# Combining two expert outputs per token: rows ordered by partition, second choice scaled on ScalarE

## The chip, the cores and the metric

The kernel is one program on one core of a Trainium2 chip. The metric is the device time of one execution in microseconds (us). A core has TensorE (PE in the profile), VectorE (DVE), ScalarE (ACT), GpSimd (POOL) and SyncE (SP), which run in parallel and meet at semaphores, and 16 DMA engines that move data between the chip's memory and the on-chip buffer of 128 partitions. SP, ScalarE and GpSimd issue the transfers.

## What is computed

The input `x` holds 128 sequences of 64 tokens with 128 channels, 8192 tokens in all, in float32. Two layers run over it, each an attention block and a feed-forward block with residuals. The change touches the end of the last block only, a mixture of 8 experts of which each token takes 2:

```python
gate_scores = jax.nn.softmax(x @ Wg + bg, axis=-1)
topk_scores, topk_idx = jax.lax.top_k(gate_scores, TOP_K)          # TOP_K = 2
topk_scores = topk_scores / (jnp.sum(topk_scores, axis=-1, keepdims=True) + 1e-08)
combine_w = jnp.einsum('bsk,bske->bse', topk_scores, onehot)
for e in range(NUM_EXPERTS):
    h = jax.nn.gelu(x @ W1[e] + b1[e])
    y = h @ W2[e] + b2[e]
    output = output + y * combine_w[..., e:e + 1]
...
x = x + output
```

Since only two of the eight weights of a token differ from zero, the kernel computes two rows of 128 outputs per token and adds them, each times its gate, to the token.

## The kernel before

Tokens live in 64 tiles of 128 (one token per partition), in 16 groups of `GT` = 4 tiles. `s.xg(g)` is the resident copy of group g, 128 partitions by 4 tiles by 128 channels in float32 (256 KB). Four stages follow each other, each closed by a barrier of all engines:

- `load_weights` and `first_layer`, to about 400 us.
- `cross_attention`, the longest stage. Beside the attention, it routes: for each group it finds the two best experts of each token and writes the normalised token twice (choice 0 and choice 1) into `moe_slots`, by indirect DMAs on GpSimd, sorted by expert. Each slot row also carries `dest`, an integer that says which row of the later output buffer belongs to this token and choice. VectorE steps `dest` once per group (line 1083), starting from a table of constants, `C_DST` (line 66, used in line 1093).
- `apply_experts`: 71 tiles of 256 slots go through the two products of their expert. SP loads a tile of slots (up to 12 ahead; before it reuses a buffer, it waits until the old tile's outputs have landed, line 1325), TensorE, ScalarE and VectorE compute, and GpSimd writes the 256 output rows of 512 bytes to `s.z` (`moe_outputs`, 16384 rows by 128 float32, 8.39 MB) with two indirect DMAs (line 1334), at the row that `dest` gives. Slots without a token carry a number beyond the buffer and are not written.
- `combine`, the last stage: for each of the 16 groups SP loads the rows of both choices from `s.z` into one of four buffers `f_z` (two DMAs of 256 KB, line 1467). VectorE does eight `scalar_tensor_tensor` (x = z * gate + x, 128 by 128 each, line 1483): four for choice 0, a `drain` (line 1485), because the next four read what these wrote, and four for choice 1. The last one counts `combined` up. ScalarE computes nothing in this stage; it waits for `combined` and issues the store of the group (256 KB, line 1473). SP waits for `combined` of group g-4 before it refills that group's buffer.

In memory the row of choice k, tile t, partition p is row (64k + t) * 128 + p. So a partition's load for one choice of a group is four pieces of 512 bytes, each 64 KB from the next, and neighbouring partitions lie side by side. The order of the work in `combine` is written out by hand: each engine runs its loop over the groups in sequence.

Of the kernel before, what the change touches and what calls it, by code (L numbers as in the profile page):

```python
# [10 lines left out]
ALU = mybir.AluOpType  # L11
ACT = mybir.ActivationFunctionType
AX = mybir.AxisListType

P = 128
BATCH, SEQ, D = 128, 64, 128
TILES = BATCH * SEQ // P
GT = 4
GROUPS = TILES // GT
# [11 lines left out]
C_TRI, C_ONE, C_DST, C_IT, C_R0, C_N0 = 1001, 1129, 1257, 1385, 1457, 1465  # L31
# [3 lines left out]
def constants():  # L35

    t, s = np.arange(SEQ), np.arange(SEQ // 2)
    w = 2 * np.pi / SEQ
    re = np.cos(w * np.outer(t, s))
    im = -np.sin(w * np.outer(t, s))  # L40
    im[:, 0] = (-1.0) ** t
    straight, turned = np.concatenate([re, im], 1), np.concatenate([im, re], 1)
    c, n = 2 * np.cos(w * np.outer(s, t)), 2 * np.sin(w * np.outer(s, t))
    a, b = c.copy(), c.copy()
    a[0], b[0] = 1.0, (-1.0) ** t
    inv, inv_turned = np.concatenate([a, b], 0) / SEQ, np.concatenate([n, -n], 0) / SEQ
    out = np.zeros((P, C_ALL))
    for u in range(2):
        here, other = slice(64 * u, 64 * u + 64), slice(64 * (1 - u), 64 * (1 - u) + 64)
        out[here, C_DQ + 64 * u:C_DQ + 64 * u + 64] = straight  # L50
        out[other, C_DK + 64 * u:C_DK + 64 * u + 64] = straight
        out[other, C_DK + P + 64 * u:C_DK + P + 64 * u + 64] = turned
        out[here, C_INV + 64 * u:C_INV + 64 * u + 64] = inv
        out[here, C_INV + P + 64 * u:C_INV + P + 64 * u + 64] = inv_turned
    out[:, C_ID:C_ID + P] = np.eye(P)
    ch = np.arange(P)
    by_parity = np.argsort(ch // 8 % 2, kind="stable")
    out[:, C_HM:C_HM + P] = ch[:, None] // 8 == by_parity[None, :] // 8

    out[ch, C_ROW + ch % 8 * 8 + ch // 16] = 1  # L60
    out[:, C_IE:C_IE + 32] = np.repeat(np.arange(8), TOP)[None]
    out[:, C_I8:C_I8 + 8] = np.arange(8)[None]
    out[:, C_DC] = ch % 8 + 64
    out[:, C_TRI:C_TRI + P] = ch[:, None] < ch[None, :]
    out[:, C_ONE:C_ONE + P] = 1
    out[:, C_DST:C_DST + 2 * TILES] = np.arange(2 * TILES)[None] * P + ch[:, None]
    out[:, C_IT:C_IT + 72] = np.arange(72)[None]
    out[:, C_R0:C_R0 + 8] = np.arange(8)[None] * BATCH * SEQ
    out[0, C_N0:C_N0 + 8] = np.arange(8) * BATCH * SEQ
    return out.astype(np.float32)  # L70
# [778 lines left out]
def cross_attention(nc, s, ctx_in, picks, tab):  # L849
# [4 lines left out]
    m = {n: sem("c_" + n) for n in names.split()}  # L854
# [4 lines left out]
    with ExitStack() as ctx:  # L859
# [144 lines left out]
        def _(dve):  # L1004
            def step(i, k):
# [74 lines left out]
                    dve.tensor_tensor(mask[:], eq[:, 0, :, :], eq[:, 1, :, :], ALU.add).then_inc(mr["mask"], 1)  # L1080
                if (g := group(i, k, ROUTE_STEP)) is not None:
                    wait(dve, scattered, 128 * g)
                    dve.tensor_scalar(dest, dest, GT * P, None, ALU.add)
                if (g := group(i, k, ROUTE_TOP)) is not None:
                    dve.drain()
                    for j in range(GT):
# [1 line left out]
                if (g := group(i, k, ROUTE_POS)) is not None:  # L1088
# [1 line left out]
                    dve.drain()  # L1090
                    dve.tensor_reduce(pf[:], pk[:], AX.X, ALU.add).then_inc(mr["pos"], 1)
                    dve.tensor_tensor(crun[:], crun[:], picked[:], ALU.add)
            dve.tensor_scalar(dest, s.dst_rows.rearrange("p (k t) -> p k t", k=2)[:, :, 0:GT], float(-GT * P), None, ALU.add)
            dve.tensor_copy(crun[:], s.count0)
            dve.memset(one8[:], 1.0)
            dve.memset(zero[:], 0.0)
# [187 lines left out]
def attend_and_route(nc, s, ctx_in, out):  # L1284

    sem = s.sem
    names = "x_t xt2 h gelu h_high h_split y y_done exp combined stored"
    m = {n: sem("d_" + n) for n in names.split()}
    x_in = [sem(f"d_x_in{n}") for n in range(XBUF)]
    y_out = [sem(f"d_y_out{n}") for n in range(YBUF)]  # L1290
# [161 lines left out]

def combine(nc, s, m, z_in, sb, gate, out):

    zt = [sb(f"f_z{n}", [P, 2, GT, D]) for n in range(4)]
    ov = out.rearrange("(t two) s d -> (two s) t d", two=2)
    zv = s.z.rearrange("(k t p) d -> p k t d", k=2, p=P)
    with nc.Block() as block:  # L1458

        @block.sync  # L1460
        def _(sp):
            for g in range(GROUPS):
                q = g % 4
                if g >= 4:
                    sp.wait_ge(m["combined"], g - 3)
                for k in range(2):
                    sp.dma_start(zt[q][:, k, :, :], zv[:, k, GT * g:GT * g + GT, :]).then_inc(z_in[q], 16)  # L1467

        @block.scalar
        def _(act):  # L1470
            for g in range(GROUPS):
                act.wait_ge(m["combined"], g + 1)
                act.dma_start(ov[:, GT * g:GT * g + GT, :], s.xg(g)).then_inc(m["stored"], 16)
            act.wait_ge(m["stored"], 16 * GROUPS)

        @block.vector
        def _(dve):
            for g in range(GROUPS):
                q = g % 4
                dve.wait_ge(z_in[q], 32 * (g // 4 + 1))  # L1480
                for k in range(2):
                    for j in range(GT):
                        last = dve.scalar_tensor_tensor(s.xg(g)[:, j, :], zt[q][:, k, j, :], gate[:, GT * g + j, k:k + 1], s.xg(g)[:, j, :], ALU.mult, ALU.add)  # L1483
                    if k == 0:
                        dve.drain()  # L1485
                last.then_inc(m["combined"], 1)

# [68 lines left out]
```

## Time and profile before

| | us |
|---|---|
| three runs: median | 1721.38 |
| three runs: lowest, highest | 1720.53, 1723.71 |
| profiled execution, its own time | 1717.49 |
| its span in the trace | 1715.7 |
| SP issues the first load of `combine` | 1672.27 |
| VectorE starts its first group | 1676.03 |
| ScalarE issues the last store | 1712.9 |

All times on the trace count from the span's start. The profile names an instruction by engine, line and the tiles it writes and reads; the chain of waits follows the work back from the last instruction, at each step to what released it. The DMA share of a stretch is the time that packets spent on the 16 engines, divided by 16 times the stretch; packets of two queues overlap on one engine, so it can be over 1. "SPq" and "ACTq" are the instruction queues of SP and ScalarE that issue DMAs. The last stage is the stretch from 1672 us on, some 43 of 1716 us.

### The profile page before, as it was taken

Reading aid. Unit: us, or ns where it says so; the run is one execution under the profiler, and the core shown is the slowest. Engines: PE = TensorE matmul, PEld = TensorE weight load, DVE = VectorE, ACT = ScalarE, POOL = GpSimd, SP = SyncE. Lnnn points to the kernel's source line nnn. Section 1 sums busy time; section 2 is a strip of 40 time slices with the busy share of each in tenths; the row PEclk is TensorE's granted clock in tenths of the full one; section 3 lists DMA queues with packets and bytes.
Section 4 is the critical chain, followed back from the end, with each engine's and each line's share of the span. In section 5 each row is a group of like instructions: output and inputs, shape, how many; then the busy total and the mean of one; then the engine's idle time right before and its main releaser. Section 6 shows DMA issues by size and latency. Waiting matters only on the chain. (4 is left out here: it accounts for less than half of the span.)

```text
span 1715.7 us, 52980 instructions
## 1 busy us (share of the span) xinstructions
PE 1451.0 (85%) x17213; PEld 1224.8 (71%) x17213; DVE 1437.1 (84%) x4166; ACT 1256.9 (73%) x3770; POOL 1093.6 (64%) x1433
## 2 busy tenths in 40 slices
PE   4888889985699999999999999999999937999960
PEld 3766677763588887787778778777877825888850
DVE  3588899996799999999999999899989835888868
ACT  1367677874699988898898888888988815666640
POOL 1466666663566577777777777777777664666650
PEclk7999999998799999999999999999999967999995
DMA  4553443400000000000000000000000002332219
GB/s 136 173 194 132 159 149 137 148 1 1 15 7 7 7 13 14 18 16 12 12 15 15 11 12 17 11 12 15 15 11 8 13 30 80 83 86 79 76 34 294
DMA packets 101783, 97.20 MB, mean 57 GB/s; under 512 B 13256, under 2 KB 87275, under 8 KB 101504
## 3 DMA queue, kind: packets, MB, share of 16 engines
q1 hardware_dynamic: 79168, 70.02, 12.8%
q0 software_dynamic: 8640, 16.87, 3.0%
q10 hardware_dynamic: 13824, 8.39, 1.7%
q8 instruction: 83, 1.36, 0.3%
q14 instruction: 68, 0.56, 0.1%
HBM read 39.32 MB, written 56.83 MB: 56 GB/s over the span
## 5 line engine op out<-in xcount | busy, mean ns | idle before, releaser
L958 POOL TENSOR_TENSOR c_p<-c_p,c_rden 128x512 f32<-128x512 f32 x256 | 266.4, 1041 | 175.6 <-DVE c_rden L1023 173.6
L1163 ACT ACTIVATE c_p<-bank,c_nmax 128x128 f32<-128x128 f32 x1024 | 362.8, 377 | 3.8 <-DVE c_nmax L1009 3.8
L1163 ACT ACTIVATION_READ_ACCUMULATOR c_p<-bank,c_nmax 128x1 f32 x1024 | 223.0, 218 | 0.0
L1334 POOL DMA_INDIRECT moe_outputs<-e_y,e_rows x142 | 153.4, 1080 | 93.4 <-DVE e_y L1363 56.4
L1009 DVE TENSOR_REDUCE c_nmax<-bank 128x4 f32<-128x512 f32 x256 | 174.4, 681 | 39.8 <-PE bank L104 36.0
L102 PE MATMUL bank<-c_kvT,qk_fused 128*128 128x128 f16 x1024 | 188.9, 222 | 1.8 <-ACT c_kvT L1142 1.4
L103 PE MATMUL bank<-c_kvT,qk_fused 128*128 128x128 f16 x1024 | 188.8, 222 | 0.0
L104 PE MATMUL bank<-c_kvT,qk_fused 128*128 128x128 f16 x1024 | 188.8, 222 | 0.0
L1230 PE MATMUL bank<-const,c_p 128*128 128x128 f32 x1024 | 156.4, 275 | 13.3 <-DVE c_pT0rest L1034 12.6
L1402 ACT ACTIVATE e_h<-bank,moe_b 128x256 f32<-128x256 f32 x284 | 118.2, 466 | 65.6 <-PE bank L104 64.2
L998 POOL DMA_INDIRECT moe_slots<-r_rows,r_pos x128 | 131.0, 1023 | 35.9 <-issue 35.9
L102 PE MATMUL bank<-vo_fused,c_o0high 128*128 128x128 f16 x512 | 93.7, 221 | 32.0 <-DVE x L1019 32.0
L1230 PEld LDWEIGHTS bank<-const,c_p 128*128 128x128 f32 x1024 | 108.2, 141 | 16.1 <-POOL c_p L958 13.8
L102 PE MATMUL bank<-vo_fused,c_o1high 128*128 128x128 f16 x512 | 92.6, 220 | 18.6 <-DVE x L1019 18.6
L102 PEld LDWEIGHTS bank<-c_kvT,qk_fused 128*128 128x128 f16 x1024 | 104.0, 102 | 3.4 <-ACT c_kvT L1142 2.3
L1147 ACT ACTIVATE c_pT0high<-bank 128x512 f16<-128x512 f32 x128 | 76.8, 600 | 34.6 <-PE bank L1230 34.1
L103 PEld LDWEIGHTS bank<-c_kvT,qk_fused 128*128 128x128 f16 x1024 | 101.8, 99 | 0.4
L104 PEld LDWEIGHTS bank<-c_kvT,qk_fused 128*128 128x128 f16 x1024 | 101.8, 99 | 0.0
L102 PE MATMUL bank<-c_kvT,c_g0high 128*128 128x128 f16 x512 | 94.5, 222 | 0.9 <-DVE c_g0rest L1028 0.6
L1028 DVE SCALAR_TENSOR_TENSOR c_g0rest<-bank,c_g0high 128x512 f16<-128x512 f32 x128 | 85.0, 664 | 11.9 <-ACT c_g0high L1137 11.8
L103 PE MATMUL bank<-c_kvT,c_g0high 128*128 128x128 f16 x512 | 94.4, 222 | 0.0
L104 PE MATMUL bank<-c_kvT,c_g0rest 128*128 128x128 f16 x512 | 94.3, 222 | 0.0
(296 smaller groups left out, 6062.6 us busy)
## 6 DMA issues: line engine op xcount, KB each, us to landing
moe_slots<-slot_fill SPq DMA_DIRECT2D x66, 516.0 KB, 5.3
e_rows<-moe_slots SPq DMA_DIRECT2D x71, 129.0 KB, 2.4
f_z<-moe_outputs SPq DMA_DIRECT2D x32, 256.0 KB, 4.8
x<-in_x SPq DMA_DIRECT2D x16, 256.0 KB, 3.1
a_ctx<-in_ctx SPq DMA_DIRECT2D x32, 128.0 KB, 3.2
moe_stage<-in_L_ffn_W ACTq DMA_DIRECT2D x16, 256.0 KB, 3.1
c_ctx<-in_ctx SPq DMA_DIRECT2D x128, 32.0 KB, 2.0
out_x<-x ACTq DMA_DIRECT2D x16, 256.0 KB, 4.7
```

The source lines that it names most:

```text
L102: pe.matmul(out, lhs[0], rhs[0], start=start, stop=False)
L103: pe.matmul(out, lhs[0], rhs[1], start=False, stop=False)
L104: return pe.matmul(out, lhs[1], rhs[0], start=False, stop=stop)
L958: pool.tensor_tensor(pr[r % 4][:], pr[r % 4][:], rep(rden[r % 4][:], 2, P), ALU.mult).then_inc(m["pn"], 1)
L998: pool.indirect_dma_start(s.xs, bass.IndirectOffsetOnAxis(ap=pos[:, c, j:j + 1], axis=0), rows[:, c, j, :], None).then_inc(scattered, 16)
L1009: dve.tensor_reduce(nmax[r % 4][:], SB[r % 2][:].rearrange("p (h c) -> p h c", h=4), AX.X, ALU.max, negate=True).then_inc(m["max"], 1)
L1028: dve.scalar_tensor_tensor(lo, GB[r % 2][:].rearrange("p (a n) -> p a n", a=2), 0.125, hi, ALU.mult, ALU.subtract).then_inc(m["g_copied"], 1)
L1147: act.activation(ptc[r % 2][0][:], PT[:], ACT.Copy).then_inc(m["pt_high"], 1)
L1163: last = act.activation(pr[r % 4][:, h, :], SB[r % 2][:, P * h:P * h + P], ACT.Exp, bias=nmax[r % 4][:, h:h + 1], accum_out=den[r % 4][:, ...
L1230: last = pe.transpose(PT[:, P * h:P * h + P], pr[r % 4][:, h, :], s.ident)
L1334: pool.indirect_dma_start(s.z, bass.IndirectOffsetOnAxis(ap=xr[t % XBUF][:, h, 2 * D:ROW].bitcast(U32), axis=0), ys[t % YBUF][:, h, :], No ...
L1402: act.activation(hf[t % 2][:, b, :], HB[b][:, 0:TSLOT], ACT.Gelu_apprx_tanh, bias=s.moe_b1[:, bass.ds(e * KB + b, 1)]).then_inc(m["gelu"], 1)
```

## The change

Three things change together.

1. The row of choice k, tile t, partition p becomes row 2 * (64p + t) + k. `C_DST` holds the new numbers, and the step of `dest` per group becomes 2 * GT in place of GT * P. Neighbouring partitions now lie 64 KB apart, and the two choices of a tile side by side.
2. A load of `combine` takes two tiles with both choices: 2 KB in succession per partition, still 256 KB per DMA and two DMAs per group.
3. ScalarE multiplies the choice-1 rows by their gates into a new buffer `f_share` (two of them), four ACTIVATEs per group, then counts `scaled` up; it issues the store of a group one group later in its own order. VectorE does the four `scalar_tensor_tensor` of choice 0, the drain, and then one `tensor_tensor` of 128 by 512 that adds `f_share`, after a wait for `scaled`.

```diff
-    out[:, C_DST:C_DST + 2 * TILES] = np.arange(2 * TILES)[None] * P + ch[:, None]
+    choice, tile = np.arange(2)[:, None], np.arange(TILES)[None, :]
+    out[:, C_DST:C_DST + 2 * TILES] = (2 * (ch[:, None, None] * TILES + tile) + choice).reshape(P, 2 * TILES)
...
-                    dve.tensor_scalar(dest, dest, GT * P, None, ALU.add)
+                    dve.tensor_scalar(dest, dest, 2 * GT, None, ALU.add)
...
-            dve.tensor_scalar(dest, s.dst_rows.rearrange("p (k t) -> p k t", k=2)[:, :, 0:GT], float(-GT * P), None, ALU.add)
+            dve.tensor_scalar(dest, s.dst_rows.rearrange("p (k t) -> p k t", k=2)[:, :, 0:GT], float(-2 * GT), None, ALU.add)
...
-    zt = [sb(f"f_z{n}", [P, 2, GT, D]) for n in range(4)]
+    zt = [sb(f"f_z{n}", [P, GT, 2, D]) for n in range(4)]
+    share = [sb(f"f_share{n}", [P, GT, D]) for n in range(2)]
     ov = out.rearrange("(t two) s d -> (two s) t d", two=2)
-    zv = s.z.rearrange("(k t p) d -> p k t d", k=2, p=P)
+    zv = s.z.rearrange("(p t k) d -> p t k d", k=2, p=P)
...
-                for k in range(2):
-                    sp.dma_start(zt[q][:, k, :, :], zv[:, k, GT * g:GT * g + GT, :]).then_inc(z_in[q], 16)
+                for half in range(2):
+                    at = GT * g + 2 * half
+                    sp.dma_start(zt[q][:, 2 * half:2 * half + 2, :, :], zv[:, at:at + 2, :, :]).then_inc(z_in[q], 16)
...
-            for g in range(GROUPS):
+            def store(g):
                 act.wait_ge(m["combined"], g + 1)
                 act.dma_start(ov[:, GT * g:GT * g + GT, :], s.xg(g)).then_inc(m["stored"], 16)
+
+            for g in range(GROUPS):
+                act.wait_ge(z_in[g % 4], 32 * (g // 4 + 1))
+                if g >= 2:
+                    act.wait_ge(m["combined"], g - 1)
+                for j in range(GT):
+                    last = act.activation(share[g % 2][:, j, :], zt[g % 4][:, j, 1, :], ACT.Copy, scale=gate[:, GT * g + j, 1:2])
+                last.then_inc(m["scaled"], 1)
+                if g:
+                    store(g - 1)
+            store(GROUPS - 1)
...
-                q = g % 4
-                dve.wait_ge(z_in[q], 32 * (g // 4 + 1))
-                for k in range(2):
-                    for j in range(GT):
-                        last = dve.scalar_tensor_tensor(s.xg(g)[:, j, :], zt[q][:, k, j, :], gate[:, GT * g + j, k:k + 1], s.xg(g)[:, j, :], ALU.mult, ALU.add)
-                    if k == 0:
-                        dve.drain()
-                last.then_inc(m["combined"], 1)
+                dve.wait_ge(z_in[g % 4], 32 * (g // 4 + 1))
+                for j in range(GT):
+                    dve.scalar_tensor_tensor(s.xg(g)[:, j, :], zt[g % 4][:, j, 0, :], gate[:, GT * g + j, 0:1], s.xg(g)[:, j, :], ALU.mult, ALU.add)
+                dve.drain()
+                dve.wait_ge(m["scaled"], g + 1)
+                dve.tensor_tensor(s.xg(g), s.xg(g), share[g % 2][:], ALU.add).then_inc(m["combined"], 1)
```

VectorE in `combine`, groups 0 to 2, in the kernel before (`f_z0` to `f_z3` are the load buffers, `d_z_in` their semaphores):

```order
L1483 SCALAR_TENSOR_TENSOR x<-f_z0,d_gate,x 128x128 [waits d_z_in0]
L1483 SCALAR_TENSOR_TENSOR x<-f_z0,d_gate,x 128x128 x7
L1483 SCALAR_TENSOR_TENSOR x<-f_z1,d_gate,x 128x128 [waits d_z_in1]
L1483 SCALAR_TENSOR_TENSOR x<-f_z1,d_gate,x 128x128 x7
L1483 SCALAR_TENSOR_TENSOR x<-f_z2,d_gate,x 128x128 [waits d_z_in2]
L1483 SCALAR_TENSOR_TENSOR x<-f_z2,d_gate,x 128x128 x7
```

The same place on VectorE in the changed kernel:

```order
L1495 SCALAR_TENSOR_TENSOR x<-f_z0,d_gate,x 128x128 [waits d_z_in0]
L1495 SCALAR_TENSOR_TENSOR x<-f_z0,d_gate,x 128x128 x3
L1498 TENSOR_TENSOR x<-x,f_share0 128x512 [waits d_scaled]
L1495 SCALAR_TENSOR_TENSOR x<-f_z1,d_gate,x 128x128 [waits d_z_in1]
L1495 SCALAR_TENSOR_TENSOR x<-f_z1,d_gate,x 128x128 x3
L1498 TENSOR_TENSOR x<-x,f_share1 128x512 [waits d_scaled]
```

Four of eight instructions of a group have gone, and one larger one with a wait of its own has come. ScalarE in `combine` before, from the barrier to the end of the stage:

```order
L1469 UNCONDITIONAL_BRANCH [waits barrier_Pool_Activation_PE_DVE_SP_release]
L1473 DMA out_x<-x 128x4x128 [waits d_combined] x16
L1458 UNCONDITIONAL_BRANCH [waits d_stored]
```

and in the changed kernel, groups 0 to 3:

```order
L1483 ACTIVATE f_share0<-f_z0,d_gate 128x128 [waits d_z_in0]
L1483 ACTIVATE f_share0<-f_z0,d_gate 128x128 x3
L1483 ACTIVATE f_share1<-f_z1,d_gate 128x128 [waits d_z_in1]
L1483 ACTIVATE f_share1<-f_z1,d_gate 128x128 x3
L1476 DMA out_x<-x 128x4x128 [waits d_combined]
L1483 ACTIVATE f_share0<-f_z2,d_gate 128x128 [waits d_combined,d_z_in2]
L1483 ACTIVATE f_share0<-f_z2,d_gate 128x128 x3
L1476 DMA out_x<-x 128x4x128 [waits d_combined]
L1483 ACTIVATE f_share1<-f_z3,d_gate 128x128 [waits d_combined,d_z_in3]
L1483 ACTIVATE f_share1<-f_z3,d_gate 128x128 x3
```

The store of group g-1 now stands behind the scaling of group g in ScalarE's queue. No table load stands among these rows. The other stages keep their instructions in their order.

## Rows read from the trace of the kernel before

**Rows 1.** Busy time by stretch: us, engines (instructions), PE clock, DMA share, GB/s

```profile
1672.00:1676.00 4.00, 0.00 (x0) 0.00 (x0) 0.00 (x0) 0.00 (x0) 0.00 (x0) 0.50 0.63 176
1676.00:1678.70 2.70, 0.00 (x0) 0.00 (x0) 2.28 (x8) 0.00 (x0) 0.00 (x0) 0.50 1.07 299
1684.00:1700.00 16.00, 0.00 (x0) 0.00 (x0) 15.43 (x57) 0.00 (x0) 0.00 (x0) 0.50 1.15 344
1706.00:1716.00 10.00, 0.00 (x0) 0.00 (x0) 6.70 (x25) 0.00 (x0) 0.00 (x0) 0.50 0.62 184
```

**Rows 2.** Timeline from 1670 us, all engines: start us, us, what [idle before]

```profile
1672.27 32.53 SPq L1467 DMA_DIRECT2D f_z<-moe_outputs  x32
1676.03 2.35 DVE L1483 SCALAR_TENSOR_TENSOR x<-f_z,d_gate,x 128x128 f32<-128x128 f32 x8 [11.69 <-DMA f_z<-moe_outputs]
1678.42 34.91 ACTq L1473 DMA_DIRECT2D out_x<-x  x16
1678.72 34.19 DVE L1483 SCALAR_TENSOR_TENSOR x<-f_z,d_gate,x 128x128 f32<-128x128 f32 x120 [0.34 <-DMA f_z<-moe_outputs]
```

**Rows 3.** Chain of waits, one group of it: start us, us, what

```profile
1684.39 0.07 issue
1684.47 0.35 DVE x L1483
1684.82 0.26 DVEq L1485
1685.08 1.57 DVE x L1483 x6
```

**Rows 4.** Who waited for whom from 1665 us: total us, times, longest

```profile
SPq L1467 <- DVE x L1483: 15.7, 12, 1.6
DVE x L1483 <- DMA f_z<-moe_outputs: 12.0, 2, 11.7
```

**Rows 5.** Loads and stores of `combine`, by tile

```profile
L1467 SPq DMA_DIRECT2D f_z<-moe_outputs x32: 360/508/1450, 1672.3 to 1704.3; - x32
DMA to landing us min/median/max: 2.9/4.8/5.6
...
L1473 ACTq DMA_DIRECT2D out_x<-x x16: 378/458/463, 1678.4 to 1712.9; - x16
```

**Rows 6.** VectorE groups by form: names, shapes, count, busy us, mean ns, idle before

```profile
L505 DVE TENSOR_TENSOR b_xc<-x,b_mv 128x512 f32<-128x512 f32 x16 | 12.3, 769 | 1.5
L493 DVE TENSOR_TENSOR x<-x,bank 128x512 f32<-128x512 f32 x12 | 8.1, 678 | 0.0
```

**Rows 7.** ScalarE groups by form

```profile
L1163 ACT ACTIVATE c_p<-bank,c_nmax 128x128 f32<-128x128 f32 x1024 | 362.8, 377 | 3.8 <-DVE c_nmax L1009 3.8
L642 ACT ACTIVATE a_spec<-bank 128x384 f32<-128x384 f32 x64 | 30.1, 489 | 26.7 <-PE bank L712 26.7
L613 ACT ACTIVATE a_kk<-bank 128x512 f32<-128x512 f32 x32 | 19.1, 596 | 25.5 <-PE bank L727 25.5
L625 ACT ACTIVATE b_junk<-b_gelu 128x512 f32<-128x512 f32 x64 | 40.3, 630 | 0.5
L632 ACT ACTIVATE a_ew<-a_ev 128x32 f32<-128x32 f32 x16 | 3.7, 229 | 9.3 <-issue 7.0 <-DVE a_ev L470 2.1
```

**Rows 8.** DMA queues, 1684 to 1700 us: packets, MB, share of 16 engines

```profile
q1 hardware_dynamic: 7379, 3.67, 76.7%
q10 hardware_dynamic: 3698, 1.84, 38.2%
```

**Rows 9.** DMA queues, 56 to 60 us; then the stretch 125 to 130 us

```profile
q10 hardware_dynamic: 138, 0.26, 16.8%
...
125.00:130.00 5.00, 5.00 (x68) 4.16 (x67) 4.85 (x18) 3.85 (x7) 3.65 (x5) 1.00 1.01 402
```

**Rows 10.** `apply_experts`: SP's waits, then the software queue in 1440 to 1660 us

```profile
SPq L1325 <- DMA moe_outputs<-e_y,e_rows: 116.2, 51, 4.8
...
q0 software_dynamic: 4352, 8.34, 11.9%
```

**Rows 11.** The last indirect stores, by tile and as queue in 1660 to 1673 us

```profile
L1334 POOL DMA_INDIRECT moe_outputs<-e_y,e_rows x142: 981/983/1499, 1437.6 to 1666.4; - x142
...
q0 software_dynamic: 160, 0.00, 0.9%
```

## What I expect of the change

> **What bounds the kernel now.** The edits outside `combine` keep every instruction; they change integers. So I read the last stage first, and then look for what the new row numbers can do to the stage before it.
>
> Start with the busy times by stretch [rows 1]: from 1684 to 1700 us VectorE is busy 15.43 of 16 us, ScalarE, TensorE and GpSimd not at all, and the DMA engines show a share of 1.15 at a flat 344 GB/s. Both VectorE and the DMA engines could be the bound, and the waits decide [rows 4]: SP waited 12 times for VectorE to free a buffer, VectorE waited for a load only twice, both at the start. The timeline [rows 2] shows one unbroken piece of 120 instructions after that. A flat 344 GB/s is just what VectorE asks for: a group moves 512 KB in and 256 KB out, 786 thousand bytes, in one VectorE period. The chain [rows 3] gives that period: 0.07 + 0.35 + 0.26 + 1.57 = 2.25 us; by the timeline it is 34.19 / 15 = 2.28. The instructions follow each other at 1.57 / 6 = 0.262 us, and the only gap is at the drain.
>
> So the path of the stage is: barrier, first load issued at 1672.27, first group at 1676.03, 2.35 us for it, 0.34 us of wait for the second load, 15 groups, VectorE's end at 1678.72 + 34.19 = 1712.91, then the last store to the span's end at 1715.7, 2.8 us.
>
> **The change part by part.**
>
> *VectorE.* Four `scalar_tensor_tensor` stay: 0.35 for the first and three more at 0.262, 1.14 us. The drain's gap of 0.07 stays. Then one addition of 128 by 512 with both inputs in the on-chip buffer. Nearest rows [rows 6]: 769 ns for L505 (both inputs there, one repeated) and 678 ns for L493 (one input in a PSUM bank). An instruction's last 0.35 - 0.262 = 0.09 us is hidden under the next one, so the step costs 0.59 to 0.68 us; I take 0.67, near L505, which has the same input memories. A passed wait for `scaled` may add up to 0.07, one more such gap; I take 0.02. Period: 1.14 + 0.07 + 0.67 + 0.02 = 1.90 us, with bounds 1.80 and 1.96. That is 0.38 less than 2.28 in each of 15 groups, and in the first group 2.35 becomes about 2.05.
>
> *ScalarE.* Four ACTIVATEs of 128 by 128 from and to the on-chip buffer. No row has this form. From above: 377 ns, the same shape with an exponential and a row sum. From below: 229 ns for 128 by 32. Between them, 384 columns take 489 and 512 take 596 ns, 0.84 ns a column, so 128 columns take 489 - 256 x 0.84 = 274, and 34 more for a source outside PSUM (630 against 596): 0.31 us [rows 7]. Four are 1.23 us (0.92 to 1.51). Behind them in the queue stands the issue of a store, 0.46 us [rows 5], and two or three waits of 0.07 at most: 1.23 + 0.46 + 0.15 = 1.84 us (1.5 to 2.1). Before the change ScalarE only issued. The store of group g-1 is behind the scaling of group g, which waits for its load; loads are ahead, so this delays no store while VectorE is the bound. VectorE's addition of group g needs a scaling that starts right after the store of group g-2: it is done some 1.84 us after VectorE's end of group g-2, and is wanted 1.90 + 1.2 us after it. So 1.84 is beside 1.90 and hidden, with little to spare. In the first group the scaling and the four VectorE steps start together, 1.23 against 1.14: 0.1 to 0.15 us exposed. A load of a function table would cost 1.3 us once; the order of instructions has none.
>
> *Loads.* Today a packet of 512 bytes takes 0.767 x 16 x 16 / 7379 us = 26.6 ns on the load queue and 26.4 on the store queue [rows 8]. A group is 1056 load and 528 store packets with the semaphore writes: (28.1 + 13.9) / 16 = 2.63 us of engine time in 2.28 us, so two queues overlap by a factor of 1.15. In the new loads a packet should be 2 KB. The trace has such packets: of the second queue's 138 in 56 to 60 us, most are 2 KB, and 0.168 x 16 x 4 / 138 us = 78 ns [rows 9]. A group then takes (256 x 0.078 + 0.4 + 13.9) / 16 = 2.14 us of engine time, which is 1.86 us with the overlap of today and 2.14 with none. VectorE wants 1.90. I take the lower half, since small store packets still stand beside large load packets in two queues, and since the loads have a lead of four groups at the start. That makes 786 KB / 1.90 us = 414 GB/s; the trace's best long stretch is 402 GB/s, writes of 4 KB pieces [rows 9]. This is the tightest place.
>
> The Trainium skill, "DMA: Bandwidth & Descriptors", section "Where 436 GB/s comes from", says that between memory and the on-chip buffer the memory's share of a core, about 358 GB/s, binds; by that a group would take 786 / 358 = 2.2 us (an estimate from the page) and most of the gain would be gone. The stretch at 402 GB/s [rows 9] speaks against it here.
>
> *SP.* Two issues per group at 0.51 us, as before [rows 5]. The wait of 15.7 us shrinks.
>
> *Start and end.* The first load's 3.8 us are mostly latency. 512 KB in larger packets may come 0.3 us sooner; I count nothing. The 0.34 us of wait for the second load goes, since the loads speed up. The end, 2.8 us, is one store, and stays.
>
> *The indirect stores of the experts' outputs.* Their rows of 512 bytes now go to places 64 KB apart per partition instead of side by side. They are the same in number; their queue took 11.9% of 16 engines in the experts' stage [rows 10]. If each took twice as long, SP would wait longer at line 1325 for a buffer that it fills 12 tiles ahead. 71 tiles take (1666.4 - 1437.6) / 70 = 3.3 us each, and VectorE reuses an output buffer after 6 tiles, 20 us, while the longest wait of SP was 4.8. And the last stores, just ahead of the barrier, carry no data (0.00 MB) [rows 11]: they belong to tiles without tokens. So I put this at nothing, up to +1.
>
> *Sum.* First group 1676.03 + 2.05, fifteen at 1.90: 1706.6. With 2.8 for the store: 1709.4, against 1715.7. The gain is **6.3 us**. The profiled execution's own time is 1717.49, the median of the runs 1721.38, 3.9 above; I subtract from the median: **1715.1 us**.
>
> **The rivals.**
>
> *DMA or ScalarE takes over as the bound.* If packets of two queues overlap less beside 2 KB loads, a group takes up to 2.14 us; if an ACTIVATE takes 377 ns, ScalarE's queue takes 2.1. Either way the period is 2.05 to 2.2: 15 times 0.08 to 0.23 of gain, plus 0.3 and 0.34 at the start, is 1.8 to 4.1, so **1717.3 to 1719.6**. For it: the share of 1.15 and the landing time of 4.8 us against 2.9 unloaded [rows 5], which is queueing already. Against: SP issues both loads of a group at once, so some queueing is in any case there. By the Trainium skill's 358 GB/s (the page above), the period would be 2.2, the far end of this case.
>
> *Slower: the pitch of 64 KB.* In the new layout all 16 DMA engines read rows whose addresses differ by multiples of 64 KB. If such reads meet in the same part of the memory, a 2 KB packet takes longer. The point from which it decides: today's period is kept when a load packet takes (2.28 x 1.15 x 16 - 14.3) / 256 = 108 ns, against 78. At 160 ns, half the rate, a group takes (41 + 14.3) / 16 / 1.15 = 3.0 us, +0.72 times 16, **about 1732**. For it: no load in the trace has such a pitch over all partitions. Against: the stores' pieces and those of today's loads already lie 64 KB apart within a partition at 26.4 ns [rows 8].
>
> The Trainium skill warns of this: "DMA: Bandwidth & Descriptors", section "Latency and other measured facts", row on HBM row pitch at large powers of two. It has 207 GB/s at a pitch of 512 KB against 214 at full rate, and 103 from 4 MB. By that list 64 KB would cost next to nothing; no row here shows it.
>
> *Nothing moves.* The addition of 128 by 512 could cost as much as four small ones, if it takes over 1 us. Both rows near it say no [rows 6].
>
> **How the numbers follow.** The forecast (period 1.80 to 2.03, gain 4.5 to 8) has 0.62, of which 0.61 lies over 3.4 us of gain. DMA or ScalarE as the bound 0.20, a third of it still over 3.4 us of gain. The pitch 0.12. Nothing moves 0.06. A measurement of this kernel can tell about 0.2%, 3.4 us, from no change. Faster by more: 0.61 + 0.07 = 0.68; within: 0.01 + 0.13 + 0.05 = 0.19; slower by more: 0.12 + 0.01 = 0.13. The range goes from 1712.5 (period 1.80, 0.8 us at the start, 0.3 for the spread of runs) to 1720.5, which takes in the second case with 0.9 for that spread, and leaves out the pitch and most of the last.
>
> **What would show it.** In the profile of the changed kernel: VectorE's addition (L1498) at 0.68 to 0.77 us, 16 of them, with no wait for ScalarE's `f_share` but in the first group; ACTIVATEs near 0.31 us; the first group at 1676 and groups at 1.90; some 400 to 415 GB/s in the middle of the stage, with a quarter of the load packets; the stage from first load to end in 37 us instead of 43.4. If the DMA engines bound, VectorE waits for `f_z` in most groups. If ScalarE does, it waits for `f_share`. If the pitch costs, load packets take over 80 ns, the landing time rises above 4.8 us, and the indirect stores' share in the experts' stage rises above 11.9%. I am wrong if the period is above 2.05.

## The result, and the profile after

The changed kernel takes 1715.68 us (median of 20 runs, 1709.87 to 1719.6) against 1719.72 us before (20 runs, 1715.16 to 1723.91). The ratio is 0.9974 with a 95% interval of 0.9964 to 0.9985: 4.5 us less, between 2.6 and 6.2 (the medians differ by 4.0). I had forecast 6.3 less. Executions of one kernel differ by up to 10 us, so from here on I read the last stage alone, from SP's first load of it to the end of the span.

The timeline of the changed kernel, all engines, its last stage (start us, us, what, idle before), beginning, one quiet stretch, one late load, and the end:

```profile
1678.72 28.27 SPq L1470 DMA_DIRECT2D f_z<-moe_outputs  x32
1682.16 1.28 ACT L1483 ACTIVATE f_share<-f_z,d_gate 128x128 f32<-128x128 f32 x4 [17.62 <-DMA f_z<-moe_outputs]
1682.16 1.14 DVE L1495 SCALAR_TENSOR_TENSOR x<-f_z,d_gate,x 128x128 f32<-128x128 f32 x4 [11.37 <-DMA f_z<-moe_outputs]
1683.47 0.69 DVE L1498 TENSOR_TENSOR x<-x,f_share 128x512 f32<-128x512 f32 x1 [0.17 <-ACT f_share L1483]
1684.33 0.40 ACT L1483 ACTIVATE f_share<-f_z,d_gate 128x128 f32<-128x128 f32 x1 [0.90 <-DMA f_z<-moe_outputs]
1684.33 1.14 DVE L1495 SCALAR_TENSOR_TENSOR x<-f_z,d_gate,x 128x128 f32<-128x128 f32 x4 [0.17 <-DMA f_z<-moe_outputs]
...
1686.25 1.13 DVE L1495 SCALAR_TENSOR_TENSOR x<-f_z,d_gate,x 128x128 f32<-128x128 f32 x4
...
1688.07 1.13 DVE L1495 SCALAR_TENSOR_TENSOR x<-f_z,d_gate,x 128x128 f32<-128x128 f32 x4
...
1696.50 1.14 DVE L1495 SCALAR_TENSOR_TENSOR x<-f_z,d_gate,x 128x128 f32<-128x128 f32 x4 [0.80 <-DMA f_z<-moe_outputs]
...
1713.27 0.69 DVE L1498 TENSOR_TENSOR x<-x,f_share 128x512 f32<-128x512 f32 x1 [0.16 <-ACT f_share L1483]
1713.99 0.38 ACTq L1476 DMA_DIRECT2D out_x<-x  x1
```

The stage goes from 1678.72 to the span's end at 1716.7: 38.0 us, where it was 43.4 [rows 2]. That this stage starts 6.45 us later than in the profile of before did not arise in the experts' stage: from the first to the last indirect store it takes 228.6 us against 228.8 [rows 11], and its first indirect store is already 6.6 us later. Ahead of it only integers differ, and I take this for the spread of executions.

| piece of the stage | before | forecast | after |
|---|---|---|---|
| first load issued to first arithmetic | 3.76 | 3.76 | 3.44 |
| first group, to the start of the second | 2.69 | 2.05 | 2.17 |
| the other 15 groups | 34.19 (2.28 each) | 28.5 (1.90 each) | 29.63 (1.98 each) |
| end of arithmetic to end of span | 2.79 | 2.8 | 2.74 |
| sum | 43.4 | 37.1 | 38.0 |

The quiet stretch shows VectorE's own new period, 1688.07 - 1686.25 = 1.82 us, less than the 1.90 of the forecast. But the mean is 1.98, and the waits of the changed kernel say why (total us, times, longest):

```profile
DVE x L1495 <- DMA f_z<-moe_outputs: 12.5, 4, 11.4
DVE x L1498 <- ACT f_share L1483: 1.4, 8, 0.2
SPq L1470 <- DVE x L1498: 14.4, 12, 2.0
```

VectorE waited for a load four times. Behind the first of these, 11.4 us until the stage had any data, the other three are 1.1 us together. Seven waits for `f_share` behind the first group add 1.2 us: ScalarE and VectorE start together on a late load, and ScalarE is done 0.17 us later. The two are the 2.3 us between 15 x 1.82 and 29.63. The chain of waits of before went through VectorE in every group after the second [rows 3]; now it goes three times through a late load, once so (start us, us, what):

```profile
1689.28 0.70 DVE x L1498
1689.98 0.02 issue
1690.00 0.32 SPq L1470
1690.32 0.04 issue
1690.36 6.12 DMA f_z<-moe_outputs
1696.47 0.03 issue
1696.50 0.45 ACT f_share L1483 x2
```

VectorE frees a buffer, SP refills it, the refill takes 6.12 us, and the group that needs it starts late. Loads are 21.0 us of the chain of this stage (4.25 at its start, then 6.12, 5.18 and 5.45), where they had been the 4.91 us at the start. The queues of the changed kernel over 16 us in the middle of the stage (packets, MB, share of 16 engines):

```profile
q1 hardware_dynamic: 2149, 3.91, 67.0%
q10 hardware_dynamic: 3967, 1.97, 41.1%
```

Four us of it, where the engines are fullest (us, engines, PE clock, DMA share, GB/s):

```profile
1698.00:1702.00 4.00, 0.00 (x0) 0.00 (x0) 3.85 (x11) 2.83 (x9) 0.00 (x0) 0.50 1.09 382
```

The load queue has 2149 packets where 7379 had been [rows 8], so the packets are 2 KB as wanted. Together the queues moved 368 GB/s in this stretch, up from 344, at a share of 1.08 instead of 1.15. The first third of the stretch is at 346 to 356 GB/s, the rest at 376 to 382.

### The profile page after: what moved, and what is told of

The parts are those of the page before. It is cut to its first block and busy times, and to the rows that moved or that the text cites. A ratio compares the mean times of both kernels' runs of the same rounds, so it can differ in the third digit from the quotient of the medians.

```text
span 1716.7 us, 52994 instructions
## 1 busy us (share of the span) xinstructions
PE 1455.5 (85%) x17197; PEld 1229.8 (72%) x17213; DVE 1430.1 (83%) x4118; ACT 1276.2 (74%) x3834; POOL 1092.2 (64%) x1433
## 5 line engine op out<-in xcount | busy, mean ns | idle before, releaser
L1148 ACT ACTIVATE c_pT0high<-bank 128x512 f16<-128x512 f32 x128 | 76.7, 599 | 35.6 <-PE bank L1231 35.0
```

What stands on the lines that cost most here:

```text
L1148: act.activation(ptc[r % 2][0][:], PT[:], ACT.Copy).then_inc(m["pt_high"], 1)
```

## The experiments

The experiments ran on three other chips than the comparison above, here called B, C and D, on which the kernel before takes 1787, 1791 and 1797 us at the median. The stage of the experts is longer there with every kernel: 275 to 305 us from the first to the last indirect store, 304.8 in a profile of before, against 228.8. The last stage is not, as the first experiment shows, and so its length can be compared across all profiles. Ratios are to the kernel before on the same chip; a kernel without a ratio was run once, for its profile.

| kernel | chip | ratio, 95% interval | last stage us | load to last VectorE end us |
|---|---|---|---|---|
| before | first | | 43.4 | 40.6 |
| before again | D | | 43.3 | |
| changed | first | 0.9974, 0.9964 to 0.9985 | 38.0 | 35.2 |
| changed again | D | | 38.6 | 35.7 |
| new rows and loads only | B | 1.0008, 0.9982 to 1.0034 | 42.6 | 39.9 |
| split arithmetic only | B | 0.9970, 0.9944 to 0.9996 | 41.8 | 39.0 |
| pitch of 68 KB | B | | 38.2 | 35.5 |
| one load per group | B | 0.9954, 0.9923 to 0.9984 | 37.9 | 35.2 |
| new transfers, no arithmetic | C | | 37.3 | |
| old transfers, no arithmetic | C | | 40.2 | |
| stores last | C | | 46.7 | 33.4 |
| eight buffers | C | 0.9964, 0.9939 to 0.9990 | 39.9 | 37.1 |
| six buffers | D | | 38.3 | 35.6 |
| eight buffers, stores from GpSimd | D | 0.9978, 0.9951 to 1.0005 | 39.5 | 34.7 |

### How steady is the stage

Two unchanged kernels, profiled once more.

> The kernel before, unchanged, profiled once more beside the next three runs. It says how far the length of the last stage (43.4 us in the first profile) varies from one execution and one chip to another. Every theory: 43.4 within 0.4 us, whatever the span; if it moves by over 1 us, the stage lengths of single profiles are no fair measure.

> The changed kernel, unchanged, profiled once more: 38.0 us for the last stage, within 0.5 (its transfers bind, so it may vary more than before's), and the earlier stages as in the kernel before on the same chip, within the spread of some 5 us from one execution to another.

Measured: 1803.9 - 1760.6 = 43.3 us, and 1775.0 - 1736.4 = 38.6 us. The stage of before repeats within 0.1 us, although the whole execution was 88 us longer. The changed one moved by 0.6 us, a bit more than expected, so differences under 0.6 us among the changed kernels tell nothing. My expectation for its earlier stages missed: they were to agree within some 5 us, and on the same chip the experts' stage alone took 281.8 us in this profile and 304.8 in that of before. The two whole executions are 29 us apart, and single executions on these chips say nothing about a gain of 4 us.

### Each half of the change alone

The theory: VectorE bounded the stage, and once it is faster the transfers do. The new rows and loads alone, with the old arithmetic:

```diff
-                    dve.scalar_tensor_tensor(s.xg(g)[:, j, :], zt[g % 4][:, j, 0, :], gate[:, GT * g + j, 0:1], s.xg(g)[:, j, :], ALU.mult, ALU.add)
-                dve.drain()
-                dve.wait_ge(m["scaled"], g + 1)
-                dve.tensor_tensor(s.xg(g), s.xg(g), share[g % 2][:], ALU.add).then_inc(m["combined"], 1)
+                for k in range(2):
+                    for j in range(GT):
+                        last = dve.scalar_tensor_tensor(s.xg(g)[:, j, :], zt[q][:, j, k, :], gate[:, GT * g + j, k:k + 1], s.xg(g)[:, j, :], ALU.mult, ALU.add)
...
+                last.then_inc(m["combined"], 1)
```

> The new row order and the 2 KB loads, with the eight scalar_tensor_tensor on VectorE as before. I read the last stage as the stretch from SP's first load of it to the end of the span: 43.4 us before, 38.0 after. Theory (VectorE was the bound before, the transfers are after): VectorE's period stays 2.27 us, no wait for loads after the second group, stage 43 us, kernel the same within 1 us; the DMA share falls from 1.15 to about 0.95. Rival (the loads were already what paced the stage, and the larger packets brought the gain): stage below 40 us.

The timeline of this kernel, VectorE in the last stage:

```profile
1742.31 36.47 DVE L1485 SCALAR_TENSOR_TENSOR x<-f_z,d_gate,x 128x128 f32<-128x128 f32 x128 [11.33 <-DMA f_z<-moe_outputs]
```

One piece of 128 instructions with no gap, 36.47 / 16 = 2.28 us a group, stage 42.6 us, ratio 1.0008. VectorE did bound. The gain of 0.8 us in the stage is, for the most part, the wait for the second load, gone, and a start 0.35 us sooner. The DMA share fell to 1.06, not to 0.95 as I had written: the 2 KB packets are dearer than I took them.

The split arithmetic alone, with the old rows and 512-byte packets:

```diff
-    zt = [sb(f"f_z{n}", [P, GT, 2, D]) for n in range(4)]
+    zt = [sb(f"f_z{n}", [P, 2, GT, D]) for n in range(4)]
...
-    zv = s.z.rearrange("(p t k) d -> p t k d", k=2, p=P)
+    zv = s.z.rearrange("(k t p) d -> p k t d", k=2, p=P)
```

> The arithmetic split between ScalarE and VectorE, with the old row order and 512-byte packets. Theory (transfers bind once VectorE takes under 2 us): 345 GB/s is what these packets give at most, so the period is 2.2 us, VectorE waits for f_z in most groups, stage 41 to 42.5 us. Rival (345 GB/s was only VectorE's demand, the packets can do more): period 1.9 to 2.0, stage 38 us, as with the whole change.

The last stage's waits of this kernel (total us, times, longest):

```profile
ACT f_share L1481 <- DMA f_z<-moe_outputs: 32.5, 16, 18.7
DVE x L1493 <- DMA f_z<-moe_outputs: 15.4, 12, 11.9
DVE x L1496 <- ACT f_share L1481: 2.2, 13, 0.2
```

VectorE waited for a load 12 times, where it had waited twice [rows 4]. The stage is 41.8 us. So the first half brings 0.8 us, the second 1.6, both together 5.4 (4.7 in the second profile): each half alone runs into the bound that the other half lifts.

### What the transfers can do alone

Two kernels leave out all arithmetic of the last stage; the output is then the tokens without the experts' part. VectorE hands a buffer back as soon as it is full, here in the kernel with the new transfers, where ScalarE keeps the stores alone:

```diff
-                for j in range(GT):
-                    dve.scalar_tensor_tensor(s.xg(g)[:, j, :], zt[g % 4][:, j, 0, :], gate[:, GT * g + j, 0:1], s.xg(g)[:, j, :], ALU.mult, ALU.add)
-                dve.drain()
-                dve.wait_ge(m["scaled"], g + 1)
-                dve.tensor_tensor(s.xg(g), s.xg(g), share[g % 2][:], ALU.add).then_inc(m["combined"], 1)
+                dve.nop().then_inc(m["combined"], 1)
```

> The same without arithmetic, with the old row order and 512-byte packets. If the overlap of two queues stays at 1.15, a group takes 2.2 to 2.3 us (345 to 355 GB/s) and the stage 40 to 41.5 us; then the old transfers were a second bound just behind VectorE, which explains why the split alone brought only 1.6 us of stage. If 512-byte packets can do more, 2.0 us a group.

> Leaves out all arithmetic of the last stage: VectorE waits for a group's load and at once counts combined up, ScalarE only issues the stores of the unchanged x; loads and stores as in the changed kernel. It measures what the transfers can do alone. The changed kernel's groups followed each other at 1.99 us. Theory (transfers bind it): the last stage is hardly shorter without arithmetic, a group every 1.95 to 2.1 us, stage 36 to 37.5 us. Rival (the hand-over of buffers between load, arithmetic and store binds, the engines have room): a group every 1.8 us or less, stage below 34.5 us.

Old transfers without arithmetic, one stretch of 4 us (us, engines, PE clock, DMA share, GB/s):

```profile
1760.00:1764.00 4.00, 0.00 (x0) 0.00 (x0) 0.00 (x0) 0.00 (x0) 0.00 (x0) 0.50 1.15 346
```

New transfers without arithmetic, likewise:

```profile
1762.90:1766.90 4.00, 0.00 (x0) 0.00 (x0) 0.00 (x0) 0.00 (x0) 0.00 (x0) 0.50 1.08 393
```

The old transfers can do 345 GB/s, that is 786 / 345 = 2.28 us a group: to the digit what VectorE took. The kernel before stood at two bounds at once, and the flat 344 GB/s that I had read as VectorE's demand [rows 1] was also all that 512-byte packets in two queues can do here. The stage without arithmetic takes 40.2 us, 3.2 less than before, and most of that is at its end. In the last 10 us of the stage the kernel before moves 1.94 MB, since its loads are all in and VectorE still works through the buffers that are full; without arithmetic it is 2.90 MB, and the 0.96 MB more are 2.8 us at 345 GB/s.

The new transfers do 390 to 393 GB/s while loads run, but that stretch holds more than its share of loads, 1.23 MB beside 0.34 MB of stores, where the work has two to one. The stores fall behind, and when the loads are in they go alone, in one queue with 512-byte packets (1777.5 to 1781.5 us, then the store issues of this kernel, shortest, median and longest in ns):

```profile
q10 hardware_dynamic: 2782, 1.38, 115.1%
L1475 ACTq DMA_DIRECT2D out_x<-x x16: 422/701/5468, 1751.1 to 1780.1; - x16
```

That is 346 GB/s at a share of 1.15, the same as two queues of such packets had. So the share of 1.15 belongs to the 512-byte packets, and not to the overlap of two queues, by which I had explained it ahead of the change and in the prediction. At two to one, the fullest stretches of the changed kernel show what the new transfers give: 380 to 382 GB/s, 2.06 us a group. The stage without arithmetic takes 37.3 us, and the changed kernel with all its arithmetic is at 38.0 (38.6). So with these transfers and four buffers the arithmetic costs 0.7 to 1.3 us on top, by single profiles: the transfers bind.

### What makes the new transfers take so long: pitch, packet, or the stores

Partitions 68 KB apart instead of 64:

```diff
+ZT = TILES + 4
...
-    out[:, C_DST:C_DST + 2 * TILES] = (2 * (ch[:, None, None] * TILES + tile) + choice).reshape(P, 2 * TILES)
+    out[:, C_DST:C_DST + 2 * TILES] = (2 * (ch[:, None, None] * ZT + tile) + choice).reshape(P, 2 * TILES)
...
-        s.z = nc.dram_tensor("moe_outputs", (2 * BATCH * SEQ, D), F32, kind="Internal").ap()
+        s.z = nc.dram_tensor("moe_outputs", (2 * P * ZT, D), F32, kind="Internal").ap()
```

> The changed kernel with the partitions' rows 68 KB apart instead of 64 KB (four unused tiles of rows per partition). If the pitch of 64 KB slows the reads (2 KB load packets measured 81 ns against the 78 that I took), the middle of the stage goes from 366 GB/s to over 390, the waits for f_z go and the stage takes 36.5 us or less. If the pitch costs nothing: 38.0 us, within 0.5.

Its queues over 16 us in the middle of the stage:

```profile
q1 hardware_dynamic: 2209, 4.03, 67.5%
q10 hardware_dynamic: 3903, 1.94, 40.4%
```

38.2 us, and 67.5% for 2209 packets against 67.0% for 2149: the pitch of 64 KB costs nothing against one of 68 KB. The rival on the slower side falls, and by the packets already: it needed 108 ns for a load packet to keep the old period, and they take 80 in the mean, semaphore writes counted in. The list of the Trainium skill ("DMA: Bandwidth & Descriptors", section "Latency and other measured facts") has a small loss at 512 KB and a large one from 4 MB; it says nothing of 64 KB. That a smaller pitch costs still less was my reading of it, and this run agrees.

One load of 512 KB per group, 4 KB in succession per partition:

```diff
-                for half in range(2):
-                    at = GT * g + 2 * half
-                    sp.dma_start(zt[q][:, 2 * half:2 * half + 2, :, :], zv[:, at:at + 2, :, :]).then_inc(z_in[q], 16)
+                sp.dma_start(zt[q][:], zv[:, GT * g:GT * g + GT, :, :]).then_inc(z_in[q], 16)
```

> The changed kernel with one load of 512 KB per group, 4 KB in succession per partition, instead of two of 256 KB. If packets' own cost binds (the 4 KB pieces early in the kernel ran at 402 GB/s), the group's DMA time falls by some 5%, the waits shrink, stage 37 to 37.5 us. If bytes or the stores bind: 38 us. Against it: VectorE's first group starts only when the whole 512 KB are in, but it waited for both halves already.

```profile
q1 hardware_dynamic: 1113, 4.09, 66.8%
q10 hardware_dynamic: 3700, 1.84, 38.3%
```

Half the packets, the same share and the same bytes (4.09 MB at 66.8%, 3.91 at 67.0%): stage 37.9 us. From 2 to 4 KB the packet's size buys nothing that a single profile can show.

With all stores after the arithmetic:

```diff
                 last.then_inc(m["scaled"], 1)
-                if g:
-                    store(g - 1)
-            store(GROUPS - 1)
+            for g in range(GROUPS):
+                store(g)
             act.wait_ge(m["stored"], 16 * GROUPS)
```

> The changed kernel with all 16 stores issued after ScalarE's last scaling, so that the loads have the engines for themselves (the stage is longer as a whole, the stores then run alone). Both theories that blame transfers or hand-over say that arithmetic then runs at VectorE's own period of 1.82 us (1.14 + 0.07 + 0.60) with no waits for f_z after the first two groups: 16 groups in 29.5 us. If waits for f_z stay, the loads themselves are too slow, at the rate of the start (512 KB per 1.45 us at 360 GB/s would be ahead of 1.82).

VectorE's last addition starts at 1776.47 and ends 33.4 us after the first load, 29.9 us after the first arithmetic; it waited for a load twice, as expected. A stretch of it:

```profile
1764.50:1768.50 4.00, 0.00 (x0) 0.00 (x0) 3.85 (x12) 2.66 (x9) 0.00 (x0) 0.50 0.89 286
```

286 GB/s of loads alone at a share of 0.89, and VectorE busy throughout: 524 / 286 = 1.83 us a group. That is what VectorE asks for, not the most that loads can do (the same kernel has 385 GB/s in two us at the start). So the loads by themselves are fast enough; it is loads and stores together that are not.

### More buffers

```diff
-    zt = [sb(f"f_z{n}", [P, GT, 2, D]) for n in range(4)]
+    zt = [sb(f"f_z{n}", [P, GT, 2, D]) for n in range(8)]
...
-                q = g % 4
-                if g >= 4:
-                    sp.wait_ge(m["combined"], g - 3)
+                q = g % 8
+                if g >= 8:
+                    sp.wait_ge(m["combined"], g - 7)
```

> The changed kernel with eight load buffers instead of four. If the transfers' bandwidth binds, SP's larger lead only moves store traffic behind load traffic: VectorE waits less for f_z, the stores land later, stage 37 to 38 us (up to 1 us shorter, since loads are done earlier and the tail of stores grows). If the time from a buffer's release to the landing of its refill (4.9 to 6.1 us against three periods) binds: no waits, period 1.82, stage 35.5 us.

Neither came: the rate rose to 391 GB/s (with 4.87 MB of loads to 1.38 of stores in that stretch, where the changed kernel has 3.91 to 1.97), VectorE waited for loads only at the start, and still the stage took 39.9 us. The timeline of this kernel from the middle of the stage:

```profile
1760.13 2.80 ACTq L1476 DMA_DIRECT2D out_x<-x  x1
...
1763.03 0.40 ACT L1483 ACTIVATE f_share<-f_z,d_gate 128x128 f32<-128x128 f32 x1 [1.73 <-DVE x L1498]
1763.14 2.81 ACTq L1476 DMA_DIRECT2D out_x<-x  x1
...
1764.34 0.69 DVE L1498 TENSOR_TENSOR x<-x,f_share 128x512 f32<-128x512 f32 x1 [1.26 <-ACT f_share L1483]
```

A store's issue, 0.42 us in the changed kernel, holds ScalarE's queue for 2.80 us from 1760.13 on. The next scaling stands behind it and starts at 1763.03, and VectorE waits 1.26 us for `f_share`; the issue of 2.81 us at 1763.14 does the same to the group after. It is 4.3 us in all. I formed a new theory: with eight groups of loads under way the stores fall so far behind that their issue blocks. Six buffers should then lie between, and stores issued by GpSimd should free ScalarE:

```diff
-            def store(g):
-                act.wait_ge(m["combined"], g + 1)
-                act.dma_start(ov[:, GT * g:GT * g + GT, :], s.xg(g)).then_inc(m["stored"], 16)
...
+        @block.gpsimd
+        def _(pool):
+            for g in range(GROUPS):
+                pool.wait_ge(m["combined"], g + 1)
+                pool.dma_start(ov[:, GT * g:GT * g + GT, :], s.xg(g)).then_inc(m["stored"], 16)
```

> The changed kernel with six load buffers. With eight the stage was 39.9 us, not shorter but longer, at 391 GB/s instead of 366, and ScalarE's queue stood for up to 2.8 us at the issue of a store, with VectorE waiting up to 1.3 us for f_share. Theory (loads that run ahead fill the DMA engines, a store's issue blocks ScalarE's queue, and scaling comes late): with six the effect is smaller, 37.5 to 39 us, between four and eight. Rival (four buffers cost the gaps between refills and the eight-buffer run was only a bad execution): 37 us or less.

> Eight load buffers, and the stores issued by the idle GpSimd instead of ScalarE. If the blocked issue on ScalarE's queue is what made eight buffers slow, VectorE no longer waits for f_share, its last addition ends after some 31 us from the first load, and the stage is near that of the transfers alone (37.3 us), 37 to 38. If the transfers' order (loads first, stores late) is what costs, the stage stays at 39 to 40. Against the changed kernel the difference of at most 1 us cannot be told in whole runs: 0.996 to 0.998 of the kernel before either way.

Six buffers: 38.3 us, with issues of up to 2.86 us and 2.6 us of waits for `f_share`. The waits lie between those of four buffers (1.4 us) and eight; the stage cannot be told from that of four (38.0 and 38.6). The kernel without arithmetic above says that the number of buffers is not itself the cause: it has four, and its issues take up to 5.47 us. What the three have in common is stores that land late, at the median after 10.9 us (six buffers), 11.9 (eight) and 12.9 (no arithmetic) in 16 us in the middle of the stage, against 7.0 in the changed kernel. Stores from GpSimd, its waits in the last stage:

```profile
ACT f_share L1479 <- DMA f_z<-moe_outputs: 28.7, 14, 18.8
POOL out_x L1486 <- DVE x L1497: 28.5, 16, 10.6
DVE x L1494 <- DMA f_z<-moe_outputs: 12.3, 3, 11.4
DVE x L1497 <- ACT f_share L1479: 1.0, 6, 0.2
```

The waits for `f_share` fell from 4.3 to 1.0 us, so the blocked issue was their cause. VectorE ends 34.7 us after the first load instead of 37.1. But I had expected 31, and the stage of 39.5 is not the 37 to 38 of my expectation: from VectorE's end at 1778.43 to the span's end at 1783.2 it takes 4.8 us, where a store by ScalarE takes 2.7. What freeing ScalarE gained, the slower last store took back. The rival of my expectation, stores that pile up behind the loads, has the right number (39 to 40) and is not the cause: in the last 6 us the engines move 108 and then 67 GB/s, so nothing is in the last store's way. From 1768 us on VectorE starts most groups as their load lands, so the transfers bind again there. Of all versions that keep the arithmetic, none has a stage shorter than the changed kernel by more than the 0.6 us of its own spread. None ran in the same comparison with it; those with both changes have ratios whose intervals overlap its own.

## Why the prediction was right or wrong, point by point

- **VectorE is the bound before: right, but half of it.** The new loads alone gave nothing (1.0008), as it says. What I missed is that the transfers stood at the very same 2.28 us a group ("old transfers, no arithmetic"). "A flat 344 GB/s is just what VectorE asks for" was true, and it was also the most that could be had. I took the absence of waits for loads as room; it was a tie.
- **VectorE's new period of 1.90: the step is 1.82.** The addition of 128 by 512 takes 0.692 us, near L493's 0.678, and not L505's 0.769 which I took for its input memories; 0.60 us of it count. The wait for `scaled` costs nothing once passed.
- **ScalarE 0.31 us an instruction: right.** Four take 1.28 us (1.23 forecast); the instruction lasts 386 ns, each follows at 0.30. What I gave to the first group alone, ScalarE being later than VectorE when both start from one load, came eight times, 0.17 us each: whenever a load is late, both start together again. That is 1.2 us behind the first group, which the sum did not have.
- **Loads: this step failed, in its size and in its overlap.** I took 78 ns for a 2 KB packet, a mean that held semaphore writes too. By the packets' own times in the traces, a 2 KB packet took 84 ns in that stretch, and in the changed kernel 84 at the median and 89 in the mean, beside 27 ns for 512 bytes and 9 for a semaphore write. And I carried over an overlap of 1.15, as a property of two queues. It is one of 512-byte packets: they have it in one queue alone (115.1%), and with 2 KB packets among them the share is 1.08 to 1.10. By my own formula, (256 x 0.084 + 14.3) / 16 / 1.08 = 2.07 us a group, the 380 GB/s of the full stretches, where I had 1.86. So the transfers, and not VectorE, set the pace.
- **Why the period is 1.98 and not 2.07:** the loads have a lead of up to four groups, and the stores land late (6.3 us, 4.7 before). Against the 1.90 of the forecast it is 15 x 0.08 = 1.1 us of the 6.3, and that is where the forecast gain in the stage was lost: 2.3 us of waits, less the 1.2 by which VectorE was faster than I had it.
- **The first rival came true in part.** It had a period of 2.05 to 2.2; the mean was 1.98. The gain of 4.5 us lies between its 1.8 to 4.1 and my 6.3, at the lower edge of the 4.5 to 8 that I gave to my own case. By its sign, VectorE waits for `f_z` in most groups, it did not come: there are four such waits, and eight for `f_share` behind late loads. But the chain of waits runs through the loads, as the rival has it. Of my own signs, the period of 1.90, the 400 to 415 GB/s, the 37 us and the absence of waits for `f_share` did not come.
- **Start: 0.32 us gained**, which I had named and counted as nothing. **End: right**, 2.74.
- **The pitch: right to leave it at a small chance.** 68 KB changed nothing. The indirect stores to their new places took 11.5% of the engines between 1440 and 1660 us, 11.9% before [rows 10]; that stage did not move on the first chip.
- **358 GB/s from the Trainium skill ("DMA: Bandwidth & Descriptors", section "Where 436 GB/s comes from"):** loads and stores together, the transfers alone did 390 to 393 GB/s, the changed kernel up to 382, and with GpSimd's stores it was 402. The measurement decides: that figure does not bind one core here.
- **The range's lower end** is 0.6 too low by its own terms: 1721.38 - 7.2 - 0.8 - 0.3 is 1713.1, not 1712.5. Nothing hangs on it.
- **The time itself was luck in part.** 1715.1 against 1715.68 looks closer than the forecast was: I subtracted from 1721.38, the median of three runs, and over 20 runs the kernel before is at 1719.72. From there 6.3 us less would be 1713.4. The gain is the thing to compare.
- **In sum** the stage gained 5.4 us in the profiles of the first chip (4.7 on chip D), the runs 4.5 with an interval of 2.6 to 6.2. The sum of 6.3 is 0.9 too much by the stage.

## What to carry to other kernels

Where an engine and the transfers both look busy, run the transfers without the arithmetic before counting a gain: a stage with no wait for loads can still be within 1% of its transfer bound, and then faster arithmetic alone brings a third of what it brings together with cheaper transfers (1.6 us against 5.4 here). When reading a rate without arithmetic, look at what is in it: a stretch with more loads than their share is faster than the whole. In this stage larger pieces paid from 512 bytes to 2 KB, and not from 2 to 4 KB. And the queue of a computing engine is a risky place for stores once they land late.

## What the runs showed of the hardware that I had not expected

- 512-byte packets stop at 345 GB/s and a share of 1.15, in two queues and both directions (with arithmetic and without), and as stores alone in one queue (346 GB/s, 115.1%). 2 KB loads with 512-byte stores reach 380 to 382 GB/s at two to one in bytes, and 390 to 393 at 3.6 to one, at a share of 1.07 to 1.10. A packet takes 27 ns with 512 bytes, 84 with 2 KB and 9 as a semaphore write. With packets of 4 KB in one queue the kernel before has a share of 1.02 and 399 GB/s (56 to 57.5 us).
- The issue of a store on ScalarE's queue takes 0.38 to 0.43 us in the changed kernel, 0.87 at the median where the stores follow each other at once (stores last), up to 2.86 us with six or eight load buffers and up to 5.47 with four and no arithmetic, and it holds what stands behind it. Eight buffers made the stage longer, 39.9 us against 38.0 and 38.6 with four; six (38.3) cannot be told from four. All three kernels with an issue of over 1 us have stores that take over 10 us to land in the middle of the stage, and with the stores on another engine ScalarE's delay went. What in the queue is full at that point, no run shows.
- GpSimd's stores of the same 256 KB went out in fewer, larger packets: 693 in 2.26 MB, of which 552 have 4 KB and 141 are semaphore writes, against 3928 in 1.95 MB from ScalarE, and the engines then reached 402 GB/s. The last one took 2 us longer to land, on engines that were nearly idle.
- What makes the experts' stage 46 to 76 us longer on the other chips was not tried and stays open. It is not the new rows: the longest is that of the kernel before. That profile has TensorE at a granted clock of 0.93 in the mean of the stage, so in part of it at the lower of its two levels (1.2 and 2.4 GHz), where the first chip has 1.00 throughout, and TensorE is busy for 246.8 us with matmuls that took 219.4. It also has 69.1 us in which VectorE at line 1345 waits for something that the profile does not name, where the first chip has none.
